# Turning the normalised rows of the feed-forward units by DVE blocks and a round trip through DRAM, within the unit ahead

## The chip, the cores and the metric

The kernel runs on one core of one Trainium2 chip, in one launch. The metric is device time in microseconds (us), here 1306.5, the median of three runs from 1306.46 to 1306.56. The engines are named as in the profile: PE (TensorE), PEld (its weight loads), DVE (VectorE), ACT (ScalarE), POOL (GpSimd) and SP (SyncE, which issues all DMAs here).

## The reference

One decoder layer on x of 16 x 100 x 512 values in float32: causal self-attention, cross-attention to a context of 361 tokens per batch, and a gated feed-forward block, each on a layer norm of the residual and added to it. The change touches the last block alone:

```
x = x + ffn(layernorm(x))
wu, wg, wd = ternary(W_up), ternary(W_gate), ternary(W_down)   # 512 -> 2048, 2048 -> 512
hidden = silu(x @ wu.T) * (x @ wg.T)
ffn = hidden @ wd.T
```

The inner dimension of the first two products is the model dimension, so the normalised rows, which lie with tokens on the partitions, have to be turned: the 512 features go to the partitions, as four slabs of 128.

## The kernel before

The 1600 rows are 13 tiles of up to 125 rows (`TW`; the last has 100), and they stay in `xres` in SBUF. The feed-forward block is worked in four units (`UB`): units 0, 1 and 2 have three tiles (375 columns), unit 3 has four (475 columns). A unit has 16 steps e (`ET`), one per 128 of the 2048 hidden features. A step is an up-and-gate pair on PE (`up_gate`, L2313, two banks of `C`, 16 matmuls), a silu on ACT (`silu`, L1116), a product on DVE (`hidden`, L1753, into `hd`), its float16 high half on ACT (`hidden_hi`, L1128, `hh`), its low half on POOL in unit 0 (L746) or on DVE later (`hidden_lo`, L1765, `hl`), and the down product on PE (`down`, L2332), which gathers into the banks `A` and `B` over the whole unit. PE runs in the order up_gate(e+1), down(e). `hd`, `hh`, `hl` and the C banks are double.

Before up_gate(u, 0) the unit's rows must lie turned and split in two float16 halves, `fh` and `fl`, of which there is one pair. While unit u runs, DVE makes the statistics of the next unit's rows (`row_stats3`, L1413), their scales in four parts (`scales3_part`, L1424 to L1429 for part 0, L1155 to L1163 for parts 1 to 3), and at e = 13 the normalised rows (`normed3`, L1441, into `xn3`). At the seam, around down(u, 14) and down(u, 15), PE transposes the tiles into C banks (`x3_turn`, L2030), ACT takes the high half (`x3_hi`, L955) once all up_gates of the unit are done, and DVE takes the low half (`x3_lo`, L1448). up_gate(u+1, 0) waits for the last low half. down(u+1, 0) overwrites the banks that `add_ffn` (L1771, DVE) adds to `xres` and so waits for it, tile by tile. In unit 0, DVE also makes ternary weights during e = 0 to 11 (`ternary`, L1404 and L1405, one half of a 128 x 2048 block each step), which up_gate and down wait for at every fourth step.

The order of the work on each engine is written out by hand, and each queue runs strictly in that order. SP issues transfers in its own order too: after the last weight block it waits for each tile's `add_ffn` and writes it out.

The same kernel already sends data on the path that the change uses: in the cross-attention, DVE turns keys in 32 x 32 blocks (L1380), SP writes them to DRAM in four transfers per tile so that the blocks land in turned order (L558), and reads them back (L567, L572).

Of the kernel before, what the change touches and what calls it, by code (L numbers as in the profile page):

```python
# [104 lines left out]
def rows_of(i):  # L105

    return min(TW, NB * S - i * TW)
# [79 lines left out]
def unit_tiles(u):  # L187

    return range(3 * u, 3 * u + 3 if u < 3 else TL)
# [27 lines left out]
def build(nc, x, wqkv, wo, wx, ctxt, wffn, gains, bcols, consts, rope, out):  # L217
    with ExitStack() as ctx:
        def sb(name, shape, dt=F32):
            return ctx.enter_context(nc.sbuf_tensor(name, shape, dt))  # L220

        def sem(name):
            return ctx.enter_context(nc.semaphore(name))
# [90 lines left out]
        xn3 = [carve([TW, DM]) for _ in range(4)]  # L314
        carve = carver(region3)
        pr = carve([S, H * S])
        carve = carver(region3)
# [11 lines left out]
        qm1 = carve([128, NT, 2, S])  # L329
        carve = carver()  # L330
        UC = unit_cols(3)
        fh = carve([128, KT, UC], F16)
        fl = carve([128, KT, UC], F16)
# [4 lines left out]


        wlate = carve([128, 9, 4, 512], BF16)  # L340
        asum = sb("asum", [128, 3, NB, 1])
        fsc = sb("fsc", [128, 16])
        statc = sb("statc", [TW, 6])
# [36 lines left out]
        kd01 = nc.dram_tensor("keys01", (2, 128, NT - TD, 2, KP), F32).ap()  # L380
        kd2 = nc.dram_tensor("keys2", (2, 128, NT - TD, KP), F32).ap()

        A = [ctx.enter_context(nc.psum_tensor(f"A{i}", [128, 512], F32)) for i in range(2)]
        B = [ctx.enter_context(nc.psum_tensor(f"B{i}", [128, 512], F32)) for i in range(2)]
        Call = ctx.enter_context(nc.psum_tensor("C", [128, 4 * 512], F32))
# [2 lines left out]
        def hidden_banks(u, e):  # L388
# [31 lines left out]
                   d_xn3=1, d_x3=1, d_hd=16, d_y=1)  # L420
        sig = {n: sem(n) for n in PER}

        def credit(eng, who):
# [4 lines left out]
        def count(name, b, n):  # L428

            return sig[name], (b + 1) * PER[name] + n  # L430
# [13 lines left out]
        g_ones = sem("g_ones")  # L444
# [24 lines left out]
        g_sum, d_fsc, d_tern = sem("g_sum"), sem("d_fsc"), sem("d_tern")  # L469

        T_UNITS = (2, 3, 5, 6)

        block = ctx.enter_context(nc.Block())

# [13 lines left out]
        def _(sp):  # L488
# [121 lines left out]
                if n == 3:  # L610
                    keys_in(NB - 1)

            for i in range(TL):
                sp.wait_ge(*count("d_y", i, 1))
                at, most = i * TW, rows_of(i) // 16 * 16
                sp.dma_start(out[at:at + most], xres[0:most, i, :]).then_inc(st_y, 16)
                sp.dma_start(out[at + most:at + rows_of(i)], xres[most:rows_of(i), i, :]).then_inc(st_y, 16)
            sp.wait_ge(st_y, 2 * 16 * TL)

        @block.gpsimd  # L620
        def _(pool):
# [129 lines left out]
        def _(act):  # L751
# [198 lines left out]
            def x3_hi(u, r, bank):  # L950
                i = unit_tiles(u)[r]
                n = rows_of(i)
                act.wait_ge(*count("pe_xT3", i, 1))
                act.wait_ge(*count("pe_up", u - 1, 16))
                act.activation(fh[:, :, r * TW:r * TW + n], bank[:, 0:KT * n].rearrange("p (k s) -> p k s", k=KT),  # L955
                               ACT.Copy).then_inc(sig["a_x3"], 1)

            w_centred(0, 0)
            x_hi(0, A[1])
# [168 lines left out]
                act.activation(hh[e % 2][:, 0:n], hd[e % 2][:, 0:n], ACT.Copy).then_inc(sig["a_hh"], 1)  # L1128

            def unit(u, last=False):  # L1130
                silu(u, 0)
# [7 lines left out]
                if not last:  # L1139
                    for r in range(2, len(unit_tiles(u + 1))):  # L1140
                        x3_hi(u + 1, r, C[r - 2])


            act.wait_ge(*count("pe_pv", NB - 1, 4))
# [4 lines left out]
        def _(dve):  # L1149
# [286 lines left out]
            def normed3(u, r):  # L1436
                i = unit_tiles(u)[r]
                n = rows_of(i)
                if u > 0:
                    dve.wait_ge(*count("pe_xT3", unit_tiles(u - 1)[-1], 1))  # L1440
                dve.tensor_scalar(xn3[r][0:n], xres[0:n, i, :], mv3[0:n, r, 0:1], rs3[0:n, r:r + 1],  # L1441
                                  ALU.subtract, ALU.mult).then_inc(sig["d_xn3"], 1)

            def x3_lo(u, r, bank):
                i = unit_tiles(u)[r]
                n = rows_of(i)
                dve.wait_ge(*count("a_x3", i, 1))
                dve.tensor_tensor(fl[:, :, r * TW:r * TW + n],  # L1448
                                  bank[:, 0:KT * n].rearrange("p (k s) -> p k s", k=KT),
                                  fh[:, :, r * TW:r * TW + n], ALU.subtract).then_inc(sig["d_x3"], 1)  # L1450

            def add_cross(i, half):
                n = rows_of(i)
# [318 lines left out]
                                             xres[0:n, i, :], ALU.mult, ALU.add).then_inc(sig["d_y"], 1)  # L1772

            def unit(u, first=False, last=False):
                if not first:
                    add_ffn(u - 1)
                    hidden(u, 0)
                tiles = [] if last else range(len(unit_tiles(u + 1)))
                for e in range(ET):
                    if not first:  # L1780
                        hidden_lo(u, e)
                    if e == ET - 1 and not first and not last:
                        x3_lo(u + 1, 1, C[1])
                    if e + 1 < ET:
                        hidden(u, e + 1)
                    if first and e < 12:
                        if e == 0:
                            ternary(5, 1)
                        ternary(6 + e // 2, e % 2)
                    if last:  # L1790
                        continue
                    if first and e in (1, 3, 5):
                        row_stats3(u + 1, (e // 2,))
                    elif not first and e in (3, 6):
                        row_stats3(u + 1, (0, 1) if e == 3 else tiles[2:])
                    elif 9 <= e <= 12:
                        scales3_part(u + 1, e - 9)
                    if e == 13:
                        for r in tiles:
                            normed3(u + 1, r)  # L1800
                    elif e == ET - 2:
                        x3_lo(u + 1, 0, C[0])
                        if first:
                            x3_lo(u + 1, 1, C[1])
                for r in tiles[2:]:
                    x3_lo(u + 1, r, C[r - 2])


            for b in range(NB):
# [6 lines left out]
        def _(pe):  # L1816
# [484 lines left out]
            def up_gate(u, e, first=False):  # L2301
                if e == 0:
                    pe.wait_ge(*count("d_x3", unit_tiles(u)[-1], 1))
                if e >= 2:
                    pe.wait_ge(*count("d_hd", u, e - 1))
                if first and e % 4 == 0:
                    pe.wait_ge(d_tern, 2 * (3 * (e // 4) + 2))
                cols = unit_cols(u)
                for half in range(2):
                    n = 0  # L2310
                    for part in (fh, fl):
# [25 lines left out]
                    ins.then_inc(sig["pe_dn"], 1)  # L2337

            def unit(u, first=False, last=False):
                if not first:  # L2340
                    up_gate(u, 0)
                for e in range(ET):
                    if e + 1 < ET and not (first and e == 0):
                        up_gate(u, e + 1, first)
                    if not last and e == ET - 2:
                        pe.wait_ge(*count("d_hd", u, ET - 1))
                        x3_turn(u + 1, 0, C[0])
                        x3_turn(u + 1, 1, C[1])
                    elif not last and e == ET - 1:
                        for r in range(2, len(unit_tiles(u + 1))):  # L2350
                            x3_turn(u + 1, r, C[r - 2])
                    down(u, e, first)


# [52 lines left out]
```

## Time and profile before

| | |
|---|---|
| median of the runs | 1306.5 us |
| the profiled execution | 1306.32 us |
| its span (first to last record) | 1304.5 us |
| feed-forward, from 1023 us to the end of the span | 281 us |
| DVE, ACT, POOL busy, whole span | 62%, 48%, 23% |

All times in the rows are counted from the span's start. The profiled execution is 1.8 us longer than its span, and it is 0.18 us under the median. A busy PE says that matmuls are in flight; consecutive records overlap a little, so intervals are read from start to start. In the timeline a row is: start, duration, engine, line, operation, output<-input, shapes, count, and in brackets how long the engine had been idle and what it waited for. Rows merge equal neighbours.

### The profile page before, as it was taken

How to read it: one execution, taken by the hardware profiler on the slowest of the kernel's cores; microseconds unless marked ns; L12 is line 12 of the kernel's file. 1: busy time of each engine (PE TensorE's matmuls, PEld its weight loads, DVE VectorE, ACT ScalarE, POOL GpSimd, SP SyncE). 2: the span in 40 equal slices, each digit the busy share in tenths (PEclk: the TensorE clock that was granted, in tenths of full speed). 3: DMA queues.
4: the chain of work that ended last, by engine and by line, in shares of the span. 5: the costliest groups of instructions: out<-in, count | busy, mean ns of one | idle time of the engine just before them, and what ended most of it. 6: DMA issues, size and time to landing. Idle time of an engine off the chain costs nothing.

```text
span 1304.5 us, 27126 instructions
## 1 busy us (share of the span) xinstructions
PE 1254.5 (96%) x10655; PEld 839.2 (64%) x10655; DVE 804.8 (62%) x1933; ACT 630.2 (48%) x1437; POOL 296.1 (23%) x294
## 2 busy tenths in 40 slices
PE   8989999999999999999999999999988999999997
PEld 7656676666666666566666666666655665666554
DVE  6897788777877787445355545555455884343423
ACT  3663354333433356377677766565664523232221
POOL 0564454344344451111111112111101121000000
PEclk9999999999999999999999999999999999999999
DMA  8202000000000012124454432422322610000000
GB/s 332 73 9 74 9 8 10 2 9 9 9 8 9 9 61 91 54 51 117 124 147 126 113 99 62 127 66 67 95 73 65 229 36 25 1 24 1 24 1 30
DMA packets 104344, 80.84 MB, mean 62 GB/s; under 512 B 81690, under 2 KB 88986, under 8 KB 101018
## 3 DMA queue, kind: packets, MB, share of 16 engines
q1 hardware_dynamic: 104218, 79.11, 19.7%
q8 instruction: 85, 1.39, 0.4%
q14 instruction: 41, 0.34, 0.1%
HBM read 64.09 MB, written 11.73 MB: 58 GB/s over the span
## 4 chain that ended last, share of the span: by engine, by line
PE 81%; DVE 7%; issue 5%; ACT 4%; POOL 2%; DMA 1%; SPq 0%; POOLq 0%; DVEq 0%; ACTq 0%
PE A L1947 18%; PE A L1847 11%; PE C L2313 10%; PE A L1910 10%; PE C L1992 6%; PE B L2011 4%; PE C L1875 3%; PE A L2332 3%; PE A L1928 3%; PE B L2332 2%; PE B L1867 2%; PE C L1892 2%; PE A L1856 2%; PE C L1831 1%; PE B L1883 1%
## 5 line engine op out<-in xcount | busy, mean ns | idle before, releaser
L1947 PE MATMUL A<-wxhl,arena 128*126 128x512 f16 x1104 | 253.5, 382 | 0.6 <-issue 0.6
L1947 PEld LDWEIGHTS A<-wxhl,arena 128*126 128x126 f16 x1104 | 145.6, 136 | 86.9 <-issue 10.8
L1847 PE MATMUL A<-arena,wxhl 128*125 128x512 f16 (+1 forms) x780 | 174.4, 380 | 1.1 <-DVE tub L1213 1.1
L928 ACT ACTIVATE arena<-C 126x1600 f32<-126x1600 f32 x96 | 144.3, 1504 | 27.8 <-PE C L1992 27.8
L657 POOL TENSOR_TENSOR arena<-arena,region 126x512 f32<-126x512 f32 (+2 forms) x59 | 60.9, 1062 | 397.4 <-DVE region L1355 397.4
L1847 PEld LDWEIGHTS A<-arena,wxhl 128*125 128x125 f16 (+1 forms) x780 | 103.8, 136 | 61.4 <-DVE tub L1213 4.9
L2313 PE MATMUL C<-arena 128*128 128x375 f16 (+1 forms) x768 | 138.8, 333 | 0.0
L821 ACT ACTIVATE region<-C,negm 100x100 f32<-100x100 f32 x256 | 84.3, 358 | 100.2 <-DVE negm L1256 100.2
L631 POOL TENSOR_TENSOR region<-tub 125x512 f32<-125x512 f32 (+1 forms) x65 | 82.5, 1269 | 219.2 <-DVE tub L1213 216.9
L1910 PE MATMUL A<-arena,stageb 128*125 128x512 f16 (+1 forms) x416 | 124.1, 380 | 2.1 <-ACT qk L893 1.3
L2313 PEld LDWEIGHTS C<-arena 128*128 128x128 bf16 x768 | 74.8, 97 | 58.8
L1753 DVE SCALAR_TENSOR_TENSOR arena<-C,fsc,arena 128x375 f32<-128x375 f32 (+1 forms) x63 | 40.0, 634 | 112.2 <-ACT arena L1116 111.8
L1116 ACT ACTIVATE arena<-C,fsc 128x375 f32<-128x375 f32 (+1 forms) x63 | 37.4, 594 | 143.2 <-PE C L2313 143.2
L1332 DVE TENSOR_REDUCE region<-region 126x32 f32<-126x512 f32 x46 | 31.3, 683 | 79.8 <-ACT region L880 79.8
L1910 PE MATMUL A<-arena,alo 128*125 128x512 f16 (+1 forms) x208 | 78.9, 379 | 0.0
L2011 PE MATMUL B<-arena 126*17 126x100 f32 (+2 forms) x2752 | 75.0, 250 | 0.0
L640 POOL TENSOR_TENSOR region<-region,rstd 125x512 f32<-125x512 f32 (+1 forms) x61 | 63.8, 1077 | 48.2 <-DVE rstd L1163 48.2
L1910 PEld LDWEIGHTS A<-arena,stageb 128*125 128x125 f16 (+1 forms) x416 | 54.7, 136 | 29.7 <-issue 1.9
L804 ACT ACTIVATE sq<-A 125x512 f32<-125x512 f32 (+1 forms) x65 | 38.9, 598 | 69.2 <-PE A L1847 69.2
L1294 DVE SCALAR_TENSOR_TENSOR arena<-arena 128x1512 f16<-128x1512 f32 x16 | 27.9, 1743 | 65.1 <-ACT arena L845 65.1
L2011 PEld LDWEIGHTS B<-arena 126*17 126x17 f32 (+2 forms) x2752 | 57.2, 97 | 14.3 <-issue 14.1
L647 POOL TENSOR_TENSOR region<-region,rinv 100x400 f32<-100x400 f32 x64 | 58.6, 921 | 21.4 <-DVE rinv L1262 21.0
(205 smaller groups left out, 2217.1 us busy)
## 6 DMA issues: line engine op xcount, KB each, us to landing
stageb<-in_wffn SPq DMA_DIRECT2D x16, 768.0 KB, 6.0
arena<-in_ctxt SPq DMA_DIRECT2D x16, 756.0 KB, 7.9
keys<-arena SPq DMA_DIRECT2D x172, 48.0 KB, 2.1
stageb<-in_wffn SPq DMA_DIRECT2D x8, 1024.0 KB, 5.4
arena<-keys SPq DMA_DIRECT2D x15, 384.0 KB, 3.8
arena<-in_wqkv SPq DMA_DIRECT2D x4, 1024.0 KB, 11.9
wxhl<-in_wffn SPq DMA_DIRECT2D x4, 1024.0 KB, 6.0
arena<-in_wx SPq DMA_DIRECT2D x3, 1024.0 KB, 7.6
```

Of the source, the lines that this page charges most:

```text
L631: pool.tensor_tensor(zb[0:n, j], tb[0:n, j % 2], ub[0:n, j % 2], ALU.add).then_inc(sig["g_w"], 1)
L640: pool.tensor_tensor(z, z, r, ALU.mult).then_inc(sig["g_z"], more)
L657: pool.tensor_tensor(t, t, r, ALU.mult).then_inc(sig[done], 2 if slot == 1 and last == 1 else 1)
L821: act.activation(pr[:, n * S:(n + 1) * S], C[g][0:S, h * S:(h + 1) * S], ACT.Exp, bias=negm[:, n:n + 1], scale=-1.0, accum_out=rsum[:, n:n ...
L928: act.activation(e[:, at:at + 2].rearrange("p f (r s) -> p r f s", r=RT), Call[0:KC, :].rearrange("p (r x) -> p r x", r=RT)[:, :, 0:4 * S] ...
L1847: ins = pe.matmul(A[j % 2][0:m, :], xp[:, k, at:at + m], wp[:, j, k, :], start=(n == 0), stop=(n == 11))
L1910: ins = pe.matmul(bank[0:m, :], ap[:, h, at:at + m], wohl[:, g, part, h % 4, :], start=(n == 0), stop=(n == 47))
L1947: ins = pe.matmul(A[(par + n) % 2][0:KC, :], xp[:, k, c * KC:(c + 1) * KC], wp[:, 1 if n < 4 else 2, k, :], start=(i == 0), stop=(i == 11))
L1992: ins = pe.matmul(C[r][0:KC, f * 2 * S:(f + 1) * 2 * S], keys, qms[b % 2][group, t].rearrange("p f s -> p (f s)"), start=True, stop=True)
L2011: ins = pe.matmul(B[1][32 * j:32 * j + VW, g * S:(g + 1) * S], v[0:rows, at:at + VW], e[0:rows, (t * NC + c) % 6, h * S:(h + 1) * S], star ...
L2313: ins = pe.matmul(hidden_banks(u, e)[half][:, 0:cols], wf[3 * (e // 4) + half][:, k, (e % 4) * 128:(e % 4 + 1) * 128], part[:, k, 0:cols], ...
L2332: ins = pe.matmul((A + B)[r][0:n, :], part[e % 2][:, r * TW:r * TW + n], wf[3 * (e // 4) + 2][:, e % 4, :], start=(e == 0 and part is hh), ...
```

## The change

In units 1 to 3 PE no longer transposes. DVE turns each tile in 32 x 32 blocks into `xts`, SP writes it to a DRAM tensor `rows` in four transfers of 32 partitions each (pieces of 32 floats, 128 bytes), reads it back into `xf` (pieces of up to 125 floats), and ACT and DVE take the halves from `xf` in SBUF instead of from PSUM. `fh` and `fl` get a second home, so that the halves of unit u+1 are made while unit u still reads its own. Everything moves ahead within the unit: scales from e = 9..12 to 3..6 (6..9 in unit 0), the normalised rows from e = 13 to 6 (9), the block turns at e = 7 and on (10 and on), one tile a step, the halves at e = 10 and on (12 and on, `halves_at`), one tile a step. At a seam PE, ACT and DVE now run on as between any two steps: up_gate(u+1, 0) stands ahead of down(u, 15), silu(u+1, 0) and hidden(u+1, 0) follow the last of unit u, and `add_ffn(u)` moves behind hidden_lo(u+1, 0). SP's order gets rows_out(1), then rows_in(0) and so on. Unit 0's own rows are turned on PE as before. POOL clears the last 32 partitions of `tub` (the home of `xn3`) once, near the end of the cross-attention, since the block turn reads all 128 partitions.

```diff
@@ sync
+            def rows_out(u, r):
+                sp.wait_ge(*count("d_xt", unit_tiles(u)[r], 1))
+                for n in range(4):
+                    block = slice(32 * n, 32 * n + 32)
+                    sp.dma_start(xd[r].rearrange("(q j) k n -> j k q n", q=4)[:, :, :, block],
+                                 xts[block, r].rearrange("j (k q i) -> j k q i", k=KT, q=4)).then_inc(xw[r], 16)
+            def rows_in(u, r):
+                n = rows_of(unit_tiles(u)[r])
+                sp.wait_ge(xw[r], 64 * (u if r < 3 else 1))
+                if u > 1 and r < 3:
+                    sp.wait_ge(*count("d_x3", unit_tiles(u - 1)[r], 1))
+                sp.dma_start(xf[:, r, :, 0:n], xd[r][:, :, 0:n]).then_inc(xr[r], 16)
+            for u in range(UB):
+                if u + 1 < UB:
+                    last = len(unit_tiles(u + 1)) - 1
+                    for r in range(last + 1):
+                        rows_out(u + 1, r)
+                        if r > 0:
+                            rows_in(u + 1, r - 1)
+                    rows_in(u + 1, last)
+                for i in unit_tiles(u):
+                    (wait for add_ffn of tile i, write it out)
@@ gpsimd, turn(b, par, end)
+                if end == 1:
+                    pool.wait_ge(*count("pe_q", TL - 1, 1))
+                    pool.wait_ge(*count("g_m", NB - 1, 1))
+                    pool.memset(tub[96:128], 0.0).then_inc(g_tail, 1)
+                    pool.wait_ge(g_tail, 1)
@@ scalar, x3_hi(u, r)
-                act.wait_ge(*count("pe_xT3", i, 1))
-                act.wait_ge(*count("pe_up", u - 1, 16))
+                    act.wait_ge(xr[r], 16 * (u if r < 3 else 1))
+                    turned = xf[:, r, :, 0:n]
+                if u > 1:
+                    act.wait_ge(*count("pe_up", u - 2, 16))
@@ scalar, unit(u)
                 for e in range(ET):
                     hidden_hi(u, e)
                     if e + 1 < ET:
                         silu(u, e + 1)
-                    if e == ET - 2 and not last:
-                        x3_hi(u + 1, 0, C[0])
-                        x3_hi(u + 1, 1, C[1])
+                    elif not last:
+                        silu(u + 1, 0)
+                    if not last and 0 <= e - halves_at(u) < len(unit_tiles(u + 1)):
+                        x3_hi(u + 1, e - halves_at(u), None)
@@ vector
+            def turn_rows(u, r):
+                dve.wait_ge(*count("d_xn3", unit_tiles(u)[r], 1))
+                if u > 1 and r < 3:
+                    dve.wait_ge(xw[r], 64 * (u - 1))
+                dve.transpose(xts[:, r], xn3[r]).then_inc(sig["d_xt"], 1)
@@ vector, unit(u): order within a step e
                     if not first:
                         hidden_lo(u, e)
+                    if e == 0 and not first:
+                        add_ffn(u - 1)
                     if e + 1 < ET:
                         hidden(u, e + 1)
+                    elif not last:
+                        hidden(u + 1, 0)
                     if first and e < 12:
                         (two ternary instructions)
+                    scales = e - (6 if first else 3)
+                    if 0 <= scales < 4:
+                        scales3_part(u + 1, scales)
+                    if scales == 3:
                         for r in tiles:
                             normed3(u + 1, r)
+                    if scales - 4 in tiles:
+                        turn_rows(u + 1, scales - 4)
+                    if e - halves_at(u) in tiles:
+                        x3_lo(u + 1, e - halves_at(u), None)
@@ tensor, unit(u)
-                    if not last and e == ET - 2:
-                        pe.wait_ge(*count("d_hd", u, ET - 1))
-                        x3_turn(u + 1, 0, C[0])
-                        x3_turn(u + 1, 1, C[1])
-                    elif not last and e == ET - 1:
-                        for r in range(2, len(unit_tiles(u + 1))):
-                            x3_turn(u + 1, r, C[r - 2])
+                    elif not last:
+                        up_gate(u + 1, 0)
                     down(u, e, first)
```

## Rows read from the trace of the kernel before

**Rows 1.** The page: busy time, share of the span and instructions of each engine.

```profile
PE 1254.5 (96%) x10655; PEld 839.2 (64%) x10655; DVE 804.8 (62%) x1933; ACT 630.2 (48%) x1437; POOL 296.1 (23%) x294
```

**Rows 2.** The chain that ended last: start, duration, engine and line, end of unit 1.

```profile
1143.21 2.55 PE C L2313 x16
...
1147.06 2.56 PE C L2313 x16
```

**Rows 3.** Timeline, PE, the seam from unit 1 to 2.

```profile
1149.45 1.02 PE L2030 MATMUL C<-cst,tub 125*128 125x125 f32 x8
...
1158.85 1.05 PE L2332 MATMUL A<-region,arena 128*125 128x512 bf16 x4
```

**Rows 4.** Timeline, PE, the seam from unit 2 to 3.

```profile
1212.77 1.02 PE L2030 MATMUL C<-cst,tub 125*128 125x125 f32 x8
...
1224.47 1.02 PE L2332 MATMUL A<-region,arena 128*125 128x512 bf16 x4
...
1229.45 1.02 PE L2332 MATMUL A<-region,arena 128*125 128x512 bf16 x4
```

**Rows 5.** Timeline, PE and DVE, the seam from unit 0 to 1.

```profile
1085.75 1.02 PE L2030 MATMUL C<-cst,tub 125*128 125x125 f32 x8
...
1086.56 0.61 DVE L1753 SCALAR_TENSOR_TENSOR arena<-C,fsc,arena 128x375 f32<-128x375 f32 x1 [1.28 <-ACT arena L1116]
...
1095.53 1.05 PE L2332 MATMUL A<-region,arena 128*125 128x512 bf16 x4
```

**Rows 6.** Timeline, unit 0, steps 10 to 12: DVE's order.

```profile
1070.59 0.61 DVE L1753 SCALAR_TENSOR_TENSOR arena<-C,fsc,arena 128x375 f32<-128x375 f32 x1 [0.24 <-ACT arena L1116]
...
1074.72 0.61 DVE L1753 SCALAR_TENSOR_TENSOR arena<-C,fsc,arena 128x375 f32<-128x375 f32 x1
...
1077.80 0.15 DVE L1161 SCALAR_TENSOR_TENSOR nwt<-rs 125x3 f32<-125x3 f32 x1
...
1078.03 1.05 PE L2332 MATMUL A<-arena 128*125 128x512 bf16 x4 [0.43 <-DVE arena L1405]
...
1078.38 0.61 DVE L1753 SCALAR_TENSOR_TENSOR arena<-C,fsc,arena 128x375 f32<-128x375 f32 x1
```

**Rows 7.** Timeline, unit 0: POOL's low half, and PE waiting for one.

```profile
1079.62 0.91 POOL L746 TENSOR_TENSOR arena<-arena 128x375 f16<-128x375 f32 x1 [2.82 <-ACT arena L1128]
...
1089.01 1.05 PE L2332 MATMUL A<-arena 128*125 128x512 bf16 x4 [0.49 <-POOL arena L746]
```

**Rows 8.** DVE: the keys' block turn (durations in ns, min/median/max; first and last start).

```profile
L1380 DVE STREAM_TRANSPOSE arena<-arena x43: 565/578/580, 572.6 to 1001.4; 128x384 f32<-128x384 f32 x43
```

**Rows 9.** Timeline, DVE, end of unit 1: normalised rows, then the low half of the hidden.

```profile
1146.93 1.45 DVE L1441 TENSOR_SCALAR tub<-xres,mv,rs 125x512 f32<-125x512 f32 x3
1148.30 0.55 DVE L1765 TENSOR_TENSOR arena<-arena 128x375 f16<-128x375 f32 x1
```

**Rows 10.** SP's queue: eight writes of turned keys, issued back to back.

```profile
906.99 5.26 SPq L558 DMA_DIRECT2D keys<-arena  x8
```

**Rows 11.** Transfers: KB each and median us from issue to landing.

```profile
keys<-arena SPq DMA_DIRECT2D x172, 48.0 KB, 2.1
arena<-keys SPq DMA_DIRECT2D x1, 168.0 KB, 2.9
arena<-keys SPq DMA_DIRECT2D x1, 102.0 KB, 5.2
```

**Rows 12.** The 15 reads of L567, 384 KB each: issue to landing.

```profile
DMA to landing us min/median/max: 3.4/3.8/4.1
```

**Rows 13.** Timeline, DVE, start of unit 2: add_ffn of two tiles.

```profile
1153.47 1.40 DVE L1771 SCALAR_TENSOR_TENSOR xres<-A,fsc,xres 125x512 f32<-125x512 f32 x2
```

**Rows 14.** PE waiting in the self-attention, and windows: stretch, busy us of PE, PEld, DVE, ACT, POOL, PEclk, DMA share, GB/s.

```profile
80.05 1.90 PE L1867 MATMUL B<-cst,region 125*128 125x125 f32 x8 [2.10 <-POOL region L640]
...
80.00:84.00 4.00, 3.84 (x20) 3.64 (x20) 3.52 (x9) 2.48 (x7) 2.12 (x2) 0.60 0.22 64
```

**Rows 15.** POOL in the last turn but one of the cross-attention.

```profile
995.96 4.11 POOL L657 TENSOR_TENSOR arena<-arena,region 126x512 f32<-126x512 f32 x4 [27.39 <-DVE region L1355]
```

More of the change, by code:

```diff
@@ L313, in build @@
         carve = carver(tub)
-        xn3 = [carve([TW, DM]) for _ in range(4)]
+        xn3 = [carve([128, DM]) for _ in range(4)]
         carve = carver(region3)
@@ L331, in build @@
         UC = unit_cols(3)
-        fh = carve([128, KT, UC], F16)
-        fl = carve([128, KT, UC], F16)
+        fh = [carve([128, KT, UC], F16)]
+        fl = [carve([128, KT, UC], F16)]
         sg = [carve([128, UC]) for _ in range(2)]
@@ L340, in build @@
         wlate = carve([128, 9, 4, 512], BF16)
+        fh.append(carve([128, KT, UC], F16))
+        fl.append(carve([128, KT, UC], F16))
+        xf = carve([128, 4, KT, TW])
+        xts = carver(alo)([128, 4, DM])
         asum = sb("asum", [128, 3, NB, 1])
@@ L381, in build @@
         kd2 = nc.dram_tensor("keys2", (2, 128, NT - TD, KP), F32).ap()
+        xd = nc.dram_tensor("rows", (4, 128, KT, 128), F32).ap()
         A = [ctx.enter_context(nc.psum_tensor(f"A{i}", [128, 512], F32)) for i in range(2)]
@@ L443, in build @@
         ld_ctx, g_zero, st_y = sem("ld_ctx"), sem("g_zero"), sem("st_y")
-        g_ones = sem("g_ones")
+        g_ones, g_tail = sem("g_ones"), sem("g_tail")
+        xw, xr = [sem(f"xw{n}") for n in range(4)], [sem(f"xr{n}") for n in range(4)]
         pe_T0, a_T0 = sem("pe_T0"), sem("a_T0")
@@ L471, in build, with halves_at @@
         T_UNITS = (2, 3, 5, 6)
+        def halves_at(u):
+            return 12 if u == 0 else 10
         block = ctx.enter_context(nc.Block())
@@ L611, in _ @@
                     keys_in(NB - 1)
[L613 to L617, printed above, removed]
+            def rows_out(u, r):
[19 more added lines that the diff above has]
+                for i in unit_tiles(u):
+                    sp.wait_ge(*count("d_y", i, 1))
+                    at, most = i * TW, rows_of(i) // 16 * 16
+                    sp.dma_start(out[at:at + most], xres[0:most, i, :]).then_inc(st_y, 16)
+                    sp.dma_start(out[at + most:at + rows_of(i)], xres[most:rows_of(i), i, :]).then_inc(st_y, 16)
             sp.wait_ge(st_y, 2 * 16 * TL)
@@ L952, in x3_hi @@
                 n = rows_of(i)
-                act.wait_ge(*count("pe_xT3", i, 1))
-                act.wait_ge(*count("pe_up", u - 1, 16))
-                act.activation(fh[:, :, r * TW:r * TW + n], bank[:, 0:KT * n].rearrange("p (k s) -> p k s", k=KT),
-                               ACT.Copy).then_inc(sig["a_x3"], 1)
+                if u == 0:
+                    act.wait_ge(*count("pe_xT3", i, 1))
+                    turned = bank[:, 0:KT * n].rearrange("p (k s) -> p k s", k=KT)
+                else:
+                    act.wait_ge(xr[r], 16 * (u if r < 3 else 1))
+                    turned = xf[:, r, :, 0:n]
+                if u > 1:
+                    act.wait_ge(*count("pe_up", u - 2, 16))
+                act.activation(fh[u % 2][:, :, r * TW:r * TW + n], turned, ACT.Copy).then_inc(sig["a_x3"], 1)
             w_centred(0, 0)
@@ L1130, in unit @@
             def unit(u, last=False):
-                silu(u, 0)
+                if u == 0:
+                    silu(0, 0)
                 for e in range(ET):
@@ L1447, in x3_lo @@
                 dve.wait_ge(*count("a_x3", i, 1))
-                dve.tensor_tensor(fl[:, :, r * TW:r * TW + n],
-                                  bank[:, 0:KT * n].rearrange("p (k s) -> p k s", k=KT),
-                                  fh[:, :, r * TW:r * TW + n], ALU.subtract).then_inc(sig["d_x3"], 1)
+                turned = xf[:, r, :, 0:n] if u else bank[:, 0:KT * n].rearrange("p (k s) -> p k s", k=KT)
+                dve.tensor_tensor(fl[u % 2][:, :, r * TW:r * TW + n], turned,
+                                  fh[u % 2][:, :, r * TW:r * TW + n], ALU.subtract).then_inc(sig["d_x3"], 1)
             def add_cross(i, half):
@@ L1774, in unit @@
             def unit(u, first=False, last=False):
-                if not first:
-                    add_ffn(u - 1)
-                    hidden(u, 0)
                 tiles = [] if last else range(len(unit_tiles(u + 1)))
+                if first:
+                    dve.sem_inc(sig["d_xt"], len(unit_tiles(0)))
                 for e in range(ET):
@@ L1781, in unit @@
                         hidden_lo(u, e)
-                    if e == ET - 1 and not first and not last:
-                        x3_lo(u + 1, 1, C[1])
+                    if e == 0 and not first:
+                        add_ffn(u - 1)
                     if e + 1 < ET:
                         hidden(u, e + 1)
+                    elif not last:
+                        hidden(u + 1, 0)
                     if first and e < 12:
@@ L1793, in unit @@
                         row_stats3(u + 1, (e // 2,))
[L1794 to L1798, printed above, removed]
+                    elif not first and e in (1, 2):
+                        row_stats3(u + 1, (0, 1) if e == 1 else tiles[2:])
+                    scales = e - (6 if first else 3)
+                    if 0 <= scales < 4:
+                        scales3_part(u + 1, scales)
+                    if scales == 3:
                         for r in tiles:
                             normed3(u + 1, r)
[L1801 to L1806, printed above, removed]
+                    if scales - 4 in tiles:
+                        turn_rows(u + 1, scales - 4)
+                    if e - halves_at(u) in tiles:
+                        x3_lo(u + 1, e - halves_at(u), None)
             for b in range(NB):
@@ L2305, in up_gate @@
                     pe.wait_ge(*count("d_hd", u, e - 1))
+                elif u > 0:
+                    pe.wait_ge(*count("d_hd", u - 1, 15 + e))
                 if first and e % 4 == 0:
@@ L2310, in up_gate @@
                     n = 0
-                    for part in (fh, fl):
+                    for part in (fh[u % 2], fl[u % 2]):
                         for k in range(KT):
@@ L2339, in unit @@
             def unit(u, first=False, last=False):
-                if not first:
-                    up_gate(u, 0)
                 for e in range(ET):
-                    if e + 1 < ET and not (first and e == 0):
-                        up_gate(u, e + 1, first)
-                    if not last and e == ET - 2:
-                        pe.wait_ge(*count("d_hd", u, ET - 1))
-                        x3_turn(u + 1, 0, C[0])
-                        x3_turn(u + 1, 1, C[1])
-                    elif not last and e == ET - 1:
-                        for r in range(2, len(unit_tiles(u + 1))):
-                            x3_turn(u + 1, r, C[r - 2])
+                    if e + 1 < ET:
+                        if not (first and e == 0):
+                            up_gate(u, e + 1, first)
+                    elif not last:
+                        up_gate(u + 1, 0)
                     down(u, e, first)
```

12 lines of the change are left out of this document (7 added, 5 removed).

## The prediction

> **What bounds the kernel now.** The page first: PE is busy for 96% of the span and no other engine for more than 62% [rows 1], so time goes only where PE waits or does work that can be dropped. The chain of waits second: in the feed-forward units 1 and 2 it lies on PE without a break, gate pairs of 2.56 us that start 3.86 us apart (1143.21, 1147.06) [rows 2]. So a down product costs 1.29 us and a step 3.85 us; in unit 3 a step is 4.98 us (1224.47 to 1229.45) [rows 4]. Then the timeline of the three seams, read from the end of up_gate(u, 15), where the PE transposes start, to down(u+1, 0). A run without a seam would need two steps there.
>
> - 1 to 2: 1149.45 to 1158.85 is 9.40 us, two steps are 7.70, excess 1.70 [rows 3].
> - 2 to 3: 1212.77 to 1224.47 is 11.70; two steps with 1.29 for each down of unit 2 and 3.26 for each pair of unit 3 (4.98 less four tiles at 0.43) are 9.10; excess 2.60 [rows 4].
> - 0 to 1: 1085.75 to 1095.53 is 9.78, excess 2.08 [rows 5].
>
> These 6.4 us, 0.5% of the time, are all that the change can take away there. Third, unit 0: DVE also makes weights. A product and its ternary pair take 3.1 us of the 3.85 (1074.72 to 1077.80), the four small pieces of a scales part 0.6, the long one 1.0 (4.13 from 1070.59 to 1074.72, less 3.1), and at the end PE already waits 0.43 us for DVE's last weights [rows 6]. Whatever is moved to an earlier step of unit 0 meets that.
>
> **Seams 1 to 2 and 2 to 3.** With transposes gone and halves ready, PE gets its steady steps: -1.70 and -2.60. What must stay hidden:
>
> The chain of a tile in units 1 and 2, from the start t of hidden at e = 7: the product holds DVE for 0.53 (its 0.61 less the overlap of records) and the block turn, 512 columns for the 384 of the keys' 0.576 us [rows 8], between 0.58 and 0.77; I take 0.74. Turned at t+1.3. SP issues a write in 0.66 us (5.26 for eight) [rows 10], four in 2.65. Those had 384 pieces of 128 bytes, these have 512; if the issue grew with the pieces it would be 0.88, and both ends are kept. rows_in(0) stands behind rows_out(1), whose tile is turned at t+5.1, so it is issued at t+7.8. Its landing: 250 KB lie between the rows of 168 KB (2.9 us) and 384 KB (3.8; 3.4 to 4.1 over 15 reads), one smaller read took 5.2 [rows 11, 12]; I take 3.3, ends 2.9 and 5.2. Data at t+11.1; ACT reaches x3_hi(0) at e = 10, t+11.5. Later tiles have more room; 5.2 us would land at t+13.0, still inside what PE forgives (the low half is due about 3.05 us after the product). No cost.
>
> DVE's order costs something at e = 6, where scales part 3 (0.6) and all normalised rows (1.45 for three, 0.48 each [rows 9]) stand between a product and the next low half. A product starts 0.81 us after its pair ends (1086.56 after 1085.75 [rows 5]), so for three tiles the low half ends at 0.81+0.53+0.6+1.4+0.55 = 3.89 and PE sees it about 0.07 later, against 3.85: +0.1. In unit 2 there are four tiles: +0.56. add_ffn, three additions at 0.70 (1.40 for two [rows 13]), runs in the first step of a unit behind the first low half (done 2.55 after the pair) and ends at 4.65; PE wants the third bank at 3.85+0.86 = 4.71. Up to 0.1 over three seams; taken 0.05. Two seams together: -1.70 - 2.60 + 0.66 + 0.05 = -3.6.
>
> **Seam 0 to 1, where I expect the loss.** DVE's order is replayed from step 6. Parts 0, 1, 2 at e = 6, 7, 8 just fit: hidden(10) starts at 1066.7 as before. At e = 9: product and weights 3.1, part 3 0.6, three normalised tiles 1.45, so hidden(11) starts at 1071.85, 1.3 us after its row of before (1070.59 [rows 6]). At e = 10: 3.1 and the first turn 0.74, hidden(12) at 1075.7. At e = 11: 3.1 and the second turn: turned at 1079.5. PE forgives about 0.7 of the lateness; it loses some 0.9 by down(12), which then starts near 1079.0 instead of 1078.03 [rows 6], and that disappears in what follows.
>
> SP: rows_out(1) is issued from 1079.5 to 1082.2, rows_in(0) right behind, landed at 1085.5. But unit 0 takes the halves only two steps after the turns (e = 12 for 10), not three. On ACT, x3_hi(0) stands at e = 12 behind silu(13), done by 1078.7, and ahead of hidden_hi(13). Queued behind this wait are hidden_hi(13), silu(14) and all after them, and DVE stands in x3_lo(0). ACT comes free at 1085.5+0.6 = 1086.1 (0.6 and, on DVE, 0.7 for 500 columns are estimates from the 0.55 of a low half of 375 [rows 9]). From the start of a product to the end of POOL's low half is 2.15 us (1078.38 to 1080.53 [rows 6, 7]), 1.51 without the product, plus 0.15 to PE: down(0, 13) starts at 1087.7. Without the wait PE would start it at 1079.0+3.85 = 1082.8. Stall: 4.9 us.
>
> Then: rows_in(1) is issued at 1085.5 (behind rows_out(2)) and lands at 1088.8, rows_in(2) at 1090.3; down(14) at 1087.7+3.85 = 1091.55 needs neither late. up_gate(1, 0) follows down(14) at 1092.85 but wants x3_lo(2), which now stands at e = 14 behind hidden(15): pair end 1091.55, product start +0.81, product 0.53, low half 0.7, PE 0.1: 1093.7, a wait of 0.85 that no transfer causes. Two pairs and a down are 6.4: down(1, 0) at 1100.1, where the trace of before has it at 1095.53 [rows 5]. So the seam costs +4.6 where its excess was 2.08.
>
> The clock. In the self-attention PE waited 2.10 us after a thin stretch; the granted clock then reads 0.60 over the next 4 us, which is the lower level, 1.2 GHz, for 80% of them, or 1.6 us of PE work lost [rows 14]. A stall of 4.9 us is longer than that wait. Part of the low stretch falls into the stall itself; I take +1.5, ends 0 and 3.2 (two such stretches).
>
> The Trainium skill says the same more strongly (TensorE: Matmul & The Clock Gate, Why this matters for your kernels): idle gaps between bursts of matmuls bring the array back to its lower clock. By that rule the loss is certain; by the rows it is likely, since a shorter wait had the fall behind it, and no longer one stands beside it to compare.
>
> The rest: the memset on POOL writes 2048 columns, as many as the four operations of 4.11 us, its upper end, and goes into the 27.39 us that POOL idles ahead of them [rows 15]; without that cover it would delay the normalised keys by its own length. SP's earlier writes meet no other traffic.
>
> The Trainium skill's DMA page (DMA: Bandwidth & Descriptors, Specifications) warns of transfers in pieces under 512 bytes, and both ways here are such. The keys' 128-byte writes landed in 2.1 us [rows 11], so no further price is entered; were the reads twice as slow as their rows, the sum would be 3 us higher.
>
> **Sum.** -3.6 + 4.6 + 1.5 = +2.5. On the profiled execution's 1306.32 us this is 1308.8. The median is 0.18 above it, so 1309.0; forecast 1308.9, 0.18% over 1306.5. A measurement of this kernel can tell about 0.2%, 2.6 us, from no change, so it lies at the edge.
>
> **Rivals.**
>
> A, the stall is there and the clock stays up. For: the one fall of the rows came in a stretch where PE had been idle before the wait too, here it comes from 96% busy; against: the length of the stall. Sum +1.0, 1307.5.
>
> B, the transfers of unit 0 are in time: faster. DVE would have to keep its old times. If hidden(12) started at 1074.4, tile 1 were turned at 1078.2, the issue took 2.65 and the read 2.9, the data would land at 1083.8 and the stall still be 3.2. So it needs transfers some 3 us quicker than all rows, or ACT's wait not holding PE. Then the seam is 0.85 longer than steady, -0.4 against before in down(1, 0), and the sum is -4.0: 1302.5. For it: only that an operation not seen here could be quicker.
>
> C, longer transfers: 0.88 us an issue and the read near 4 us. Before rows_in(0) stand four issues, +0.9, and +0.7 for the landing; tile 1 then is late too. +2, and a second low stretch of the clock, +1: 1312.0. For: nothing shows a 512-piece transfer. It decides from a landing of ACT's data after 1086.5 on.
>
> D, DVE suffers more: the block turn and x3_lo now read SBUF beside POOL and units 1 and 2 lose 0.5 at several steps. Four to six steps at 0.3: +1.5, 1310.5. Against: in units 1 to 3 POOL is idle.
>
> **How the numbers follow.** Forecast with stall and low clock (1307.8 to 1310.3) 0.48; A 0.22; B 0.08; C 0.12; D 0.10. Range 1305.0 to 1311.5: from A with a stall of 3.2 to nearly C. Slower by over 0.2% means over 1309.1: four tenths of the forecast's case, C and D, 0.41; faster 0.08; same 0.51.
>
> **What would show it.** Right: no L2030 rows after 1023 us but unit 0's; seams 1 to 2 and 2 to 3 in steady steps; a wait of 4 to 6 us ahead of the down product of step 13 of unit 0, put down to POOL or ACT, with ACT's x3_hi behind a DMA; a granted clock of half behind it; 0.85 us ahead of up_gate(1, 0), behind DVE. Wrong: ACT's first x3_hi without a wait (B), issues of L558's kind over 0.8 us (C), waits at the ends of steps 7 in unit 2 of more than 0.6 us (D), or a seam in units 2 and 3 that is still there, which would take away the -4.3.

## The result

The changed kernel is slower: 1312.36 us in the median of six executions against 1306.69, ratio 1.0035 with a 95% interval of 1.002 to 1.0049; measured again beside the experiments, 1311.83 against 1306.87, ratio 1.0033 (1.002 to 1.0045). The medians by themselves lie 0.43% and 0.38% apart. The median of 1312.36 is 0.9 us above the range of the prediction (1305.0 to 1311.5); the ratio 1.0035 applied to its 1306.5 gives 1311.1, inside the range. Over all runs below, single executions lie far apart, 1309.0 to 1315.7 for the change and 1304.4 to 1312.5 for the kernel before, with standard deviations of 1.8 and 1.7 us. The profiled execution took 1310.02 us over a span of 1308.2, where [rows 1] belong to 1306.32 and 1304.5.

The page of the changed kernel, busy time by engine, answers to [rows 1]; only the 40 transposes are gone from PE:

```profile
PE 1253.0 (96%) x10615; PEld 834.1 (64%) x10615; DVE 809.9 (62%) x1943; ACT 630.4 (48%) x1437; POOL 297.8 (23%) x295
```

The two later seams of the changed kernel, PE's timeline (columns as ahead of the prediction), answer to [rows 3, 4]:

```profile
1160.48 1.02 PE L2389 MATMUL A<-arena 128*125 128x512 bf16 x4
...
1164.33 1.02 PE L2389 MATMUL A<-region,arena 128*125 128x512 bf16 x4
...
1187.43 1.02 PE L2389 MATMUL A<-arena 128*125 128x512 bf16 x4
...
1192.10 1.05 PE L2389 MATMUL A<-arena 128*125 128x512 bf16 x4 [0.66 <-DVE arena L1820]
...
1219.07 1.02 PE L2389 MATMUL A<-arena 128*125 128x512 bf16 x4
...
1228.16 1.02 PE L2389 MATMUL A<-region,arena 128*125 128x512 bf16 x4
```

down(1, 15) to down(2, 0) is 3.85 us, a plain step; down(2, 14) to down(3, 0) is 9.09, the two steps without a seam. In between stands the one step of 4.67 (1187.43 to 1192.10), from down(2, 6) to down(2, 7), behind the four normalised tiles. DVE in this step, the normalised tiles and then the low half that PE waits for:

```profile
1189.58 1.92 DVE L1489 TENSOR_SCALAR tub<-xres,mv,rs 125x512 f32<-125x512 f32 x4 [0.27 <-DVE rs L1207]
1191.41 0.54 DVE L1820 TENSOR_TENSOR arena<-arena 128x375 f16<-128x375 f32 x1
```

Unit 0 of the changed kernel, all engines, steps 10 to 15, answers to [rows 5 to 7]; L1497 is the block turn, L629 and L638 the way to and from DRAM, L1001 and L1504 the halves, L1808 hidden:

```profile
1075.43 1.05 PE L2389 MATMUL A<-arena 128*125 128x512 bf16 x4 [0.41 <-POOL arena L786]
1076.29 0.70 DVE L1497 STREAM_TRANSPOSE alo<-tub 128x512 f32<-128x512 f32 x1
...
1077.02 6.25 SPq L629 DMA_DIRECT2D rows<-alo  x8
...
1079.96 0.70 DVE L1497 STREAM_TRANSPOSE alo<-tub 128x512 f32<-128x512 f32 x1
1080.18 1.05 PE L2389 MATMUL A<-arena 128*125 128x512 bf16 x4 [0.71 <-DVE arena L1449]
...
1081.50 2.72 PE L2370 MATMUL C<-arena 128*128 128x375 f16 x16
1083.32 0.63 SPq L638 DMA_DIRECT2D arena<-rows  x1
...
1086.64 0.62 ACT L1001 ACTIVATE arena<-arena 128x500 f16<-128x500 f32 x1 [6.56 <-DMA arena<-rows]
...
1087.16 0.50 ACT L1173 ACTIVATE arena<-arena 128x375 f16<-128x375 f32 x1
1087.29 0.68 DVE L1504 TENSOR_TENSOR arena<-arena 128x500 f16<-128x500 f32 x1 [5.53 <-ACT arena L1001]
...
1087.74 0.99 POOL L786 TENSOR_TENSOR arena<-arena 128x375 f16<-128x375 f32 x1 [8.79 <-ACT arena L1173]
...
1088.88 1.94 PE L2389 MATMUL A<-arena 128*125 128x512 bf16 x4 [4.66 <-POOL arena L786]
...
1096.16 2.73 PE L2370 MATMUL C<-arena,early 128*128 128x375 f16 x16 [0.60 <-DVE arena L1504]
```

The reader follows the chain upward from PE's wait of 4.66 us ahead of down(0, 13): POOL's low half had to wait for ACT, ACT stood 6.56 us in x3_hi of tile 0 until the read of 1083.32 had landed, and that read stood behind the eight writes of tiles 0 and 1. (The trace is 1.28 us behind that of the kernel before where the block begins, at 1024.65 for 1023.37.) The four matmuls behind the wait last 1.94 us instead of 1.05.

Windows of the changed kernel behind the stall (PEclk is the number ahead of the last two), as in [rows 14]:

```profile
1086.00:1089.00 3.00, 0.12 (x1) 0.15 (x2) 1.29 (x2) 1.49 (x3) 0.99 (x1) 0.87 0.71 132
1089.00:1092.00 3.00, 3.00 (x9) 1.55 (x10) 0.68 (x1) 1.03 (x2) 0.93 (x1) 0.56 0.43 126
```

Since executions differ before the feed-forward block too, the block is best read on its own clock, from the start of up_gate(0, 0). This table holds start times on PE, all from the timelines of the profiled executions. In the kernel before and in r4, down(0, 15) stands ahead of up_gate(1, 0), in the others behind it, so the row of down(0, 15) compares only kernels with the same order:

| us after up_gate(0, 0) | before | after | r2 fill | r3 read first | r4 hybrid | r5 late |
|---|---|---|---|---|---|---|
| down(0, 12) | 54.66 | 55.53 | 55.54 | 55.52 | 54.65 | 55.53 |
| down(0, 13) | 58.53 | 64.23 | 64.23 | 62.09 | 58.52 | 59.40 |
| down(0, 15) | 65.64 | 74.08 | 72.73 | 74.86 | 65.64 | 70.67 |
| down(1, 0) | 72.16 | 77.93 | 76.58 | 78.86 | 72.16 | 74.52 |
| down(2, 0) | 135.48 | 139.68 | 138.33 | 140.61 | 133.79 | 136.27 |
| down(3, 0) | 201.10 | 203.51 | 202.17 | 204.45 | 196.78 | 200.11 |
| end of the span | 281.13 | 283.55 | 282.12 | 284.47 | 276.78 | 280.08 |

These are repeatable: three profiles of the kernel before ended at 281.13, 281.10 and 281.08, four of the changed one at 283.55 to 283.87.

### The profile page after: what moved, and what is told of

Same layout as the page of the kernel before. It is cut to its first block, busy times and chain, and to the rows that moved or that the text cites. A ratio compares the mean times of both kernels' runs of the same rounds, so it can differ in the third digit from the quotient of the medians.

```text
span 1308.2 us, 27115 instructions
## 1 busy us (share of the span) xinstructions
PE 1253.0 (96%) x10615; PEld 834.1 (64%) x10615; DVE 809.9 (62%) x1943; ACT 630.4 (48%) x1437; POOL 297.8 (23%) x295
## 4 chain that ended last, share of the span: by engine, by line
PE 81%; DVE 6%; issue 5%; ACT 3%; POOL 2%; DMA 1%; SPq 1%; DVEq 0%; POOLq 0%; ACTq 0%
PE A L2002 18%; PE A L1902 11%; PE C L2370 10%; PE A L1965 10%; PE C L2047 6%; PE B L2066 4%; PE C L1930 3%; PE A L2389 3%; PE A L1983 3%; PE B L2389 2%; PE B L1922 2%; PE C L1947 2%; PE A L1911 2%; PE B L1938 1%; PE C L1886 1%
## 5 line engine op out<-in xcount | busy, mean ns | idle before, releaser
L1808 DVE SCALAR_TENSOR_TENSOR arena<-C,fsc,arena 128x375 f32<-128x375 f32 (+1 forms) x63 | 39.9, 633 | 109.2 <-ACT arena L1161 108.4
```

## The experiments

**r1, r8, r9: the changed kernel again.** No edit.

> The changed kernel once more, for more executions beside the next three. Theory (T): in unit 0 ACT stands at x3_hi of tile 0 until its transfer has landed, PE loses 4.7 us ahead of down(0, 13), and after that stall the granted clock falls for 3 to 7 us; how much of the low stretch meets matmuls differs from run to run. Median 1310 to 1313.5 us, single executions 3 us or more apart. Rival R1: the surplus over the forecast comes from elsewhere (the memset, the cross-attention). Rival R2: DVE's fuller order in unit 0 makes the loss, the transfers would be in time without it.

Measured 1311.83 (1308.96 to 1315.68, 12 executions), ratio 1.0033 (1.002 to 1.0045). In the profile down(0, 13) starts at 64.17, down(0, 15) at 74.35, and the end comes at 283.81. The median and the spread are as T had it. The spread, though, is as wide in the kernel before, so it says nothing for the stall.

> The changed kernel unchanged, for a third profile of the same stall. T: down(0, 13) again 64.2 us after up_gate(0, 0), as in the two profiles so far (64.23, 64.17); down(0, 15), which shows what the clock took, at 74.1 (1.35 us lost) or later, up to 75.8 where the low stretch falls wholly behind the stall or comes twice. The executions' surplus of 3.2 us over r2_fill's (means of 18 and 12) wants such profiles; if all stay at 1.35 to 1.7, some of the surplus lies elsewhere.

> The same once more: a fourth profile of the stall. T: down(0, 13) at 64.2, down(0, 15) between 74.1 and 75.8.

down(0, 13) at 64.15 and 64.12, down(0, 15) at 74.34 and 74.27, ends 283.87 and 283.75; single times 1312.38 and 1311.44. In all four profiles the low stretch took 1.35 to 1.7 us (10.15 to 10.19 us from down(0, 13) to down(0, 15) in three of them and 9.85 in the first, against 8.50 in r2 below), once, never twice. So nothing in four profiles says that it varies enough to be why the median lies higher than the block's growth, as T had it.

**r2: PE filled during the stall.**

```diff
             def down(u, e, first=False):
+                if u == 0 and e == 13:
+                    for _ in range(28):
+                        pe.matmul(B[1][:, 0:375], wf[0][:, 0, 0:128], fh[0][:, 0, 0:375], start=True, stop=True)
                 pe.wait_ge(*count("a_hh", u, e + 1))
```

> 28 matmuls of 375 columns into the unused bank B[1] stand ahead of the wait of down(0, 13): 28 x 0.16 = 4.5 us of work inside the stall of 4.7 us. Their result is not used. T: down(0, 13) starts where it did, the clock stays at its upper level there, the low stretch's loss (1.7 us in the profiled run, more in others) goes: median 1308 to 1310, executions within 1.5 us. If the clock has no share: 1310 to 1313 as r1_again.

Measured 1308.53 (1307.39 to 1311.07, 12 executions), ratio 1.0012 (1.0002 to 1.0022). Its block begins 2.53 us later on the trace's clock (1027.18 for 1024.65), so down(0, 13) starts at 1091.41; these are the windows around it:

```profile
1089.00:1092.00 3.00, 2.80 (x17) 1.62 (x16) 1.29 (x2) 1.49 (x3) 1.00 (x1) 1.00 0.60 137
1092.00:1095.00 3.00, 3.00 (x20) 1.77 (x18) 0.68 (x1) 1.03 (x2) 0.93 (x1) 1.00 0.30 89
```

PE does 28 useless matmuls more and the kernel gets faster. down(0, 13) starts at 64.23 as without them, and down(0, 15) 1.35 us earlier: the granted clock stays at 1.00, where the idle PE got 0.56 over three us. That is the clock's price by itself, 1.35 us against the profile of the change and 1.65 to 1.69 against its three repeats. The median fell by 3.3 us, more than that; and the executions lie 3.7 us apart where 1.5 were expected, so the spread comes from other places too.

**r3: the read of a tile ahead of the next tile's writes.**

```diff
                     for r in range(last + 1):
                         rows_out(u + 1, r)
-                        if r > 0:
-                            rows_in(u + 1, r - 1)
-                    rows_in(u + 1, last)
+                        rows_in(u + 1, r)
```

> SP issues rows_in(r) right behind rows_out(r), for all units. T: tile 0's read is issued when its own writes have landed, 1081.2 instead of 1083.3 on the trace's clock, down(0, 13) starts 2.1 us earlier; but tiles 1 and 2 are then written and read strictly one after the other and land no earlier, so up_gate(1, 0) comes only 0.9 us earlier. Time 0.5 to 2 us under r1_again. R2: no change, since DVE's order is the same.

Measured 1310.86 (1307.21 to 1312.61), ratio 1.0023 (1.001 to 1.0035). Timeline of r3:

```profile
1080.63 0.56 SPq L638 DMA_DIRECT2D arena<-rows  x1
...
1083.98 0.62 ACT L999 ACTIVATE arena<-arena 128x500 f16<-128x500 f32 x1 [4.43 <-DMA arena<-rows]
...
1086.22 1.05 PE L2387 MATMUL A<-arena 128*125 128x512 bf16 x4 [2.53 <-POOL arena L784]
...
1093.51 0.62 ACT L999 ACTIVATE arena<-arena 128x500 f16<-128x500 f32 x1 [2.64 <-DMA arena<-rows]
...
1094.90 4.30 PE L2368 MATMUL C<-arena,early 128*128 128x375 f16 x16 [2.51 <-DVE arena L1502]
```

The first stall shrinks by 2.14 us with DVE's order untouched, so R2 is out: the wait is made by SP's order and the transfers. But tile 2 is now read so late that up_gate(1, 0) waits 2.51 us, the clock falls there instead (the pair takes 4.30 us for 2.73), and the block ends 0.9 us later than in the profile of the change, at 284.47. The expectation missed that second wait: I had 0.9 us of gain in the block. The medians go the other way, 1310.86 against 1311.83, but the two intervals overlap, and single executions of r3 lie 5.4 us apart. The profile also has two waits of nearly one length with different outcomes: behind the 2.53 us ahead of down(0, 13) the granted clock stays at 1.00 over the next three us (1086 to 1089), behind the 2.51 us ahead of up_gate(1, 0) it is 0.64 (1095 to 1098).

**r5: the halves one step later in unit 0.**

```diff
+            if u == 0:
+                return {13: (0,), 14: (1, 2)}.get(e, ())
+            return (e - 10,) if 0 <= e - 10 < len(unit_tiles(u + 1)) else ()
```

The function gives the tiles whose halves are made at step e; ACT and DVE both follow it.

> The changed kernel, only with unit 1's halves one step later: x3_hi and x3_lo of tile 0 at e = 13, of tiles 1 and 2 both at e = 14. T (ACT's queue position is what turns the transfer's latency into a stall): no wait ahead of down(0, 13); 1.0 us ahead of down(0, 14), 2.5 us ahead of up_gate(1, 0), where tile 2's read ends; from up_gate(0, 0) to the end 280.2 us for 283.6, median about 3 us under the changed kernel, 1308 to 1309. R2 (DVE's order): the loss stays near 283.

Measured 1307.00 (1305.98 to 1309.58, 11 executions), ratio 0.9998 (0.9989 to 1.0006): no difference from the kernel before can be told. Timeline of r5:

```profile
1088.94 1.05 PE L2392 MATMUL A<-arena 128*125 128x512 bf16 x4 [0.80 <-POOL arena L788]
...
1092.83 2.73 PE L2373 MATMUL C<-arena,early 128*128 128x375 f16 x16 [2.41 <-DVE arena L1507]
```

Waits of 0.80 and 2.41 us where 1.0 and 2.5 were expected, block 280.08 for 280.2; the median lies below the 1308 to 1309 expected. The transfers take as long as before; only the places where they are waited for have changed, x3_hi in ACT's queue and x3_lo, which follows it, in DVE's. With that more than the whole loss of the block is gone: 3.5 us, of which 1.35 are the clock's, since no low stretch comes in r5, not even behind its wait of 2.41 us (the pair takes 2.73). The edit moves ACT and DVE together; that ACT's wait is the one that held PE is read from the chain in the profile above (DMA, ACT, POOL, PE).

**r4: unit 1 as before, units 2 and 3 by way of DRAM.** Its core, on DVE and SP:

```diff
             for u in range(UB):
-                if u + 1 < UB:
+                if 0 < u and u + 1 < UB:
...
+                    if first:
+                        if 9 <= e <= 12:
+                            scales3_part(1, e - 9)
+                        elif e == 13:
+                            for r in tiles:
+                                normed3(1, r)
...
+                    if scales - 3 in tiles:
+                        normed3(u + 1, scales - 3)
```

> Unit 1's rows are turned on PE at the seam with everything as before the change; only units 2 and 3 take the way through DRAM; their normalised rows are made one tile a step (e = 6, 7, ...) instead of all at e = 6. T: seam 0 to 1 as before (9.78 us from the end of up_gate(0, 15) to down(1, 0)), seams 1 to 2 and 2 to 3 in steady steps, no wait at step 7: 1306.5 - 1.7 - 2.6 + 0.1 = 1302.3 us, executions within 0.7 us or so. R1: 1303.5 to 1306, with the same spread as r1_again, since the memset is still there.

Measured 1304.74 (1301.26 to 1305.41, 12 executions) against 1306.87, ratio 0.9974 (0.9962 to 0.9987): faster than both kernels. The block is 4.35 us shorter, as 1.7, 2.6 and nothing lost at the steps 7 make. PE around step 7 of unit 2 in r4, plain steps of 3.85 where the change has 4.67:

```profile
1175.96 1.02 PE L2408 MATMUL A<-arena 128*125 128x512 bf16 x4
...
1179.81 1.02 PE L2408 MATMUL A<-arena 128*125 128x512 bf16 x4
...
1183.66 1.02 PE L2408 MATMUL A<-arena 128*125 128x512 bf16 x4
```

Its median gained 2.1, not 4.3, and its executions lie 4.2 us apart, not 0.7: 1304.74 is in the range that the expectation gave to R1, a cost outside the block. So r6 and r7 test the memset.

**r6: the kernel before with the memset alone.**

```diff
+                if end == 1:
+                    pool.wait_ge(*count("pe_q", TL - 1, 1))
+                    pool.wait_ge(*count("g_m", NB - 1, 1))
+                    pool.memset(tub[96:128], 0.0).then_inc(g_tail, 1)
+                    pool.wait_ge(g_tail, 1)
```

> The kernel before with the change's POOL memset of tub[96:128] and its wait alone added. In the profiled runs the feed-forward block explains +2.4 us of the changed kernel's median surplus of 5 and -4.35 us of r4_hybrid's, which gained 2.1. T: POOL is idle there (27 us), so nothing: within 0.5 us of the kernel before, and the rest is the clock's chance in the key wait of the cross-attention. R1 (the memset costs): +1 to +2.3 us.

Measured 1307.86 against 1307.70, ratio 1.0004 (0.9992 to 1.0017); block 281.23. No effect can be told from the medians; an effect of up to 2 us is within the interval. The profiles are finer: near 1001 us PE waits 1.15 to 1.16 us for DVE (L1514 in the changed kernel) in all nine profiles with this memset and 1.08 to 1.09 in the four without it. So its price on PE is 0.07 us.

**r7: r4 with a small memset, early, in place of the large one.**

```diff
+            pool.wait_ge(*count("g_p", NB - 1, 4))
+            pool.memset(tub[96:128, 2000:2048], 0.0).then_inc(g_tail, 1)
+            pool.wait_ge(g_tail, 1)
```

> r4_hybrid with the memset cut to the 48 columns that nothing else ever writes, and put at the start of the cross-attention. T: from up_gate(0, 0) to the end 276.8 us as in r4_hybrid, median within 0.7 us of it (1304.7), lower only by chance. R1: 1302.3 to 1303, the full gain.

Measured 1305.01 (1303.57 to 1306.80, 9 executions), ratio 0.9974 (0.9965 to 0.9984); block 276.84. As r4, so the memset is not what the median of r4 lacks.

**r10, r11: the kernel before, two more profiles.**

> The kernel before, for a second profile. All profiles with the memset but one, and none of the kernel before (there is one), show the granted clock falling in the key wait of the cross-attention near 980 us. T: chance, so the kernel before shows it too in about every second profile; from up_gate(0, 0) to the end 281.1 us. R1 (the change brings it): never.

> The same, a third profile of the kernel before. T: a fall near 980 or 1015 us in one of the two; 281.1 us from up_gate(0, 0) to the end.

Single times 1306.53 and 1307.54, blocks 281.10 and 281.08. Windows near 980 us, first the changed kernel:

```profile
976.00:980.00 4.00, 1.49 (x17) 1.02 (x18) 1.70 (x4) 0.57 (x2) 1.18 (x1) 0.87 0.88 247
```

and r10, the kernel before:

```profile
976.00:980.00 4.00, 2.34 (x20) 1.50 (x21) 1.58 (x4) 1.32 (x1) 0.00 (x0) 0.83 0.97 323
```

r11 has its fall near 1015 us. The low stretch in the key waits of the cross-attention comes in both kernels, in some executions and not in others, and so does one near 80 us: that is a part of the common spread. (The expectation counted all profiles with the memset but one; by the windows it is all but two, r1 and r4.)

## Why the prediction came out as it did

The direction and the mechanism held; the size did not. I forecast 1308.9, a rise of 2.4 us, and gave no change the larger chance (0.51, against 0.41 for slower). Measured is 0.33 to 0.35% more, so slower, and the medians are 5.7 us apart, more than twice the rise that was forecast. The sum for the feed-forward block was right; the step from the block to the whole kernel was not.

- **Seams 1 to 2 and 2 to 3.** Right. Between down(1, 0) and down(3, 0) the change saves 3.4 us of the block (128.94 to 125.58), the forecast had 3.6. No transfer was late there.
- **The normalised rows at e = 6.** Three tiles cost 0.13 us (forecast 0.1), four cost 0.82 (forecast 0.56). The four take 1.92 us, 0.48 each as taken; what the sum lacked is the gap of 0.27 us ahead of the first, which DVE does not have in unit 1. Why it stands there is not shown. r4 takes both costs away by one tile a step. PE's wait of 0.66 us here meets the sign given for rival D (over 0.6), but D's mechanism is not there: the block turns take 0.70 us and x3_lo 0.68, as taken, and apart from these two steps every step of units 1 and 2 is 3.85 us.
- **DVE in unit 0.** down(0, 12) comes 0.87 us later in the block (forecast 0.9). The block turn takes 0.70 us (0.74 taken).
- **The stall.** Data landed 3.3 us after the read's issue (3.3 taken; median of nine such reads 3.2), the issue of a write took 0.63 and did not grow with the pieces; the stall was 4.66 us (4.9), the wait ahead of up_gate(1, 0) 0.60 (0.85). r5 shows that it hangs on where the wait stands in the queues, r3 that SP's order sets when it ends. Rival B, transfers in time, is out. So is C, longer transfers: the data landed at 1086.64, past its mark of 1086.5, but on the clock of the trace before that is 1085.4, where 1085.5 was forecast.
- **The clock.** Fall and price right: 1.35 to 1.7 us in four profiles, 1.5 taken, and r2 shows it apart. Rival A, the clock stays up, is out. The Trainium skill's rule (TensorE: Matmul & The Clock Gate, Why this matters for your kernels), that idle gaps between bursts of matmuls bring the lower clock, holds for this stall in 4 of 4 profiles. For shorter waits the runs show both: the fall comes behind 2.51 us in r3 and not behind 2.53 us in the same profile, nor behind 2.41 us in r5; in the kernel before, seams with waits under a microsecond never show it.
- **The sum for the block** was +2.5 us; the profiles show +2.4 to +2.8. Some of this is luck: in the first profile the two later seams gave 0.2 us less than forecast and the first cost 0.2 less (4.4 for 4.6, without the clock), which cancel.
- **The step that failed** is the one from the block to the median: "On the profiled execution's 1306.32 us this is 1308.8. The median is 0.18 above it". It took three executions within 0.1 us of each other as the kernel's spread, and put everything ahead of the block at nothing, the memset with a reason (POOL idles there), the rest with none. Over all 72 executions of the kernel before the mean is 1307.6, over 20 of the change 1312.0, a difference of 4.4 us with a standard error of 0.44. The block accounts for 2.6 of it; some 1.7 us do not lie in the block, as R1 had it.

What these 1.7 us are stays open in the main. The profiles have them too: up_gate(0, 0) starts at 1023.37, 1023.60 and 1024.62 us in the kernel before and at 1024.65, 1024.99, 1025.95 and 1026.73 in the changed one. Two small parts are the same every time. The memset costs 0.07 us. And near 463 us PE falls back by 0.35 us in all nine profiles of the changed kernel and its variants, and in none of the four of the kernel before and r6: DVE stands there for 0.31 us ahead of a piece of work of its own (L1255) with nothing that the profile shows to wait for, and PE then waits 0.23 us for DVE. What makes DVE stand is not shown. The rest lies where profiles of one kernel differ as well: in the first 18 us, by up to 2.0 us, and in the low stretches near 80, 980 and 1015 us. Three and four profiles cannot tell it from chance. Against the means of their own rounds the variants leave less over than the changed kernel's 1.9 in r1: 0.4 in r2, -0.1 in r3, 0.8 in r4, 0.4 in r5, 1.0 in r7, each with a standard error of 0.4 to 0.6, and 0.3 in r6, which has the memset alone.

## What to carry to other kernels

A transfer's latency costs nothing where its consumer stands late enough in every in-order queue; counted in steps, three were enough here and two were not, and one step's delay of the wait was worth 3.5 us. Before work is moved earlier in a stage, look what that stage's helper engine already carries: unit 0, with its weights on DVE, should have kept its old seam, and the version that does, and that makes the normalised rows one tile a step, is 0.26% faster than the kernel before. A wait on PE of 4.7 us had the clock's price on top of it in four of four profiles; useless matmuls in it paid for themselves. And before a change of a fifth of a per cent is forecast, take more than three executions to learn what the kernel's own spread is.

## What the runs showed of the hardware

A kernel's executions on one core can lie 7 us apart with identical order of work. The mean granted clock goes with it: over 62 executions of the kernel before it runs from 0.999 to 0.992 while the time runs from 1304.4 to 1312.5 us (correlation -0.86). PE waits of 1.5 to 3 us are followed by the lower clock in some executions only: of three profiles of the kernel before, one has it behind the key wait near 980 us, 2.49 us long there, one behind a wait of 1.57 us near 1015 us, one in neither place; without it the key wait was 2.68 and 2.89 us long, so a longer wait there did not bring it. The block of the kernel before, which has no such waits, repeats within 0.05 us. Issuing a DMA whose pattern has 512 pieces of 128 bytes took 0.63 us, one with 384 pieces 0.62, and its landing 2.2 us against 2.1.
